# A macaron transformer block on one core: small VectorE intermediates put into the shared PSUM banks, and the plan of the order given new costs

## The reference

```python
x = x + 0.5 * ffn(layernorm(x), w_gate, w_up, w_down)
x = x + attn(layernorm(x), Wq, Wk, Wv, Wproj, lq1, lk1, lq2, lk2)
x = x + 0.5 * ffn(layernorm(x), w_gate, w_up, w_down)

# ffn, hidden width 704; q() is a blockwise FP4 quantise and dequantise over 16 features
h = silu(q(x) @ q(w_gate).T) * (q(x) @ q(w_up).T)
out = q(h) @ q(w_down).T
# q(): scale = max(max|block| / 6, 1e-12); round |v| / scale to 0, .5, 1, 1.5, 2, 3, 4, 6

# attn: differential attention, 8 heads, 2 x 8 query and key heads of width 16
q, k = rotary(rmsnorm(q)), rotary(rmsnorm(k))
a = softmax(causal(q @ k.T / 4))          # 16 maps of 2048 x 2048 for each batch
a = a[:, :, 0] - lam * a[:, :, 1]
out = layernorm(a @ v) * (1 - LAMBDA_INIT) @ Wproj.T    # layernorm over each head's 32
```

## Time and profile before

| what | value |
|---|---|
| three runs | 2467.5, 2468.85, 2469.09 us (median 2468.85) |
| the profiled execution, its own time | 2471.45 us |
| its span, first to last instruction | 2469.5 us |
| mean granted TensorE clock | 0.937 |
| instructions | 39323 |

### The profile page before, as it was taken

One profiled execution on the slowest core, in us unless ns is written; L12 is line 12 of the kernel. 1 busy time (PEld: TensorE's weight loads), 2 busy tenths in 40 slices (PEclk: granted clock), 3 DMA queues, 4 the chain that ended last, 5 costly groups with the idle time before them and its releaser, 6 DMA issues.

```text
span 2469.5 us, 39323 instructions
## 1 busy us (share of the span) xinstructions
PE 2099.7 (85%) x13502; PEld 839.6 (34%) x13502; DVE 1831.3 (74%) x3615; ACT 1777.8 (72%) x2660; POOL 1658.3 (67%) x1520
## 2 busy tenths in 40 slices
PE   1567999899897889899998889989898889998965
PEld 1233433233333333333333333333333333332322
DVE  6888787668758888777858888886867888873434
ACT  2345677978875778778786778877787677887852
POOL 3887666766756687876766677886776677862415
PEclk8788999999998999999998999999999999998986
DMA  3122322221312132232321322223241223221101
GB/s 92 34 40 55 65 49 49 47 53 30 68 39 52 19 63 50 56 66 44 55 58 19 53 48 63 60 33 71 33 84 21 47 32 79 49 50 34 33 1 41
DMA packets 409906, 119.36 MB, mean 48 GB/s; under 512 B 390638, under 2 KB 409454, under 8 KB 409710
## 3 DMA queue, kind: packets, MB, share of 16 engines
q1 hardware_dynamic: 409710, 116.86, 25.1%
HBM read 11.96 MB, written 8.39 MB: 8 GB/s over the span
## 4 chain that ended last, share of the span: by engine, by line
PE 45%; DVE 20%; ACT 8%; POOL 5%; issue 5%; DMA 2%; SPq 1%; ACTq 0%; DVEq 0%; POOLq 0%
PE psum_o L1365 11%; PE shared L1311 10%; PE shared L1324 7%; PE psum_s L1347 7%; ACT probs L1074 6%; PE shared L1332 4%; PE shared L1379 3%; DVE nwt L473 2%; DVE nwt L472 2%; DVE h L1166 1%; PE shared L1300 1%; DMA q_stack<-st_q 1%; DVE nwt L474 1%; POOL grid L965 1%; POOL hq L961 1%
## 5 line engine op out<-in xcount | busy, mean ns | idle before, releaser
L1074 ACT ACTIVATE probs<-psum_s 128x1024 f32<-128x1024 f32 (+3 forms) x1280 | 1092.0, 896 | 234.2 <-PE psum_s L1347 170.9
L1365 PE MATMUL psum_o<-probs,v_sb 128*32 128x512 f32 (+3 forms) x5120 | 590.6, 546 | 9.5 <-POOL probs L995 8.9
L1311 PE MATMUL shared<-w_gu_T,xT 128*128 128x480 f16 (+1 forms) x2304 | 522.6, 371 | 68.5 <-DMA xT<-x 44.4
L1347 PE MATMUL psum_s<-q_stack,k_stack 64*128 64x512 f16 (+3 forms) x2560 | 431.7, 359 | 113.6 <-ACT probs L1074 97.1
L1324 PE MATMUL shared<-w_down_T,hT 128*128 128x256 f16 (+1 forms) x2176 | 315.5, 292 | 77.3 <-DVE hq L1156 55.9
L1347 PEld LDWEIGHTS psum_s<-q_stack,k_stack 64*128 64x128 f16 x2560 | 110.1, 93 | 652.6 <-ACT probs L1074 465.9
L1311 PEld LDWEIGHTS shared<-w_gu_T,xT 128*128 128x128 f16 x2304 | 207.1, 99 | 352.7 <-issue 119.4
L995 POOL TENSOR_SCALAR_AFFINE_SELECT probs<-probs 128x512 f32<-128x512 f32 x256 | 172.6, 679 | 225.7 <-ACT probs L1074 224.4
L961 POOL TENSOR_TENSOR hq<-grid,hq 128x704 f32<-128x704 f32 x128 | 222.7, 1740 | 99.8 <-ACT grid L1019 99.7
L1009 ACT ACTIVATE hq<-shared,tanh_scale 128x240 f32<-128x240 f32 (+1 forms) x384 | 172.6, 454 | 155.7 <-PE shared L1311 143.9
L1324 PEld LDWEIGHTS shared<-w_down_T,hT 128*128 128x128 f16 (+1 forms) x2176 | 204.1, 103 | 193.5 <-issue 76.6
(11 more groups left out here) (120 smaller groups left out, 2848.2 us busy)
## 6 DMA issues: line engine op xcount, KB each, us to landing
xb<-L_attn_x SPq DMA_DIRECT2D x16, 512.0 KB, 4.0
out<-xb SPq DMA_DIRECT2D x16, 512.0 KB, 3.3
hT<-h SPq DMA_TRANSPOSE x128, 3.5
xT<-x SPq DMA_TRANSPOSE x64, 3.1
k_stack<-st_k SPq DMA_TRANSPOSE x64, 3.3
q_stack<-st_q SPq DMA_TRANSPOSE x64, 3.3
k_stack<-L_ffn_w_down SPq DMA_DIRECT2D x1, 704.0 KB, 8.7
k_stack<-L_ffn_w_gate SPq DMA_DIRECT2D x1, 480.0 KB, 4.6
```

What stands on the lines that cost most here:

```text
L1074: nc.scalar.activation(probs[:, s % 3, 2 * u:2 * u + 2, q0:CHUNK], psum_s[u][:, :, q0:CHUNK], ACT.Exp, scale=HD ** -0.5 / QK_SCALE ** 2).t ...
L1311: last = nc.tensor.matmul(bank(e)[:, 0:2 * (hi - lo)], xs[:, x, t % 2, k, :], w_gu_T[:, w, k, 2 * lo:2 * hi], start=n == 0, stop=n == len( ...
L1347: last = nc.tensor.matmul(psum_s[u][:, j, q0:CHUNK], k_stack[half, at, h, kt % NTC * P:(kt % NTC + 1) * P], q_stack[half, c % 2, h, q0:CHU ...
L1365: last = nc.tensor.matmul(psum_o[at:at + VD, q0:CHUNK], v_sb[:, kt // NTC % SLOTS * NTC + kt % NTC, 2 * g + u, :], probs[:, s % 3, 2 * u + ...
```

## The change

The costs and due times of the plan are replaced, and the model of time is refined: a stage may overlap a little with the next on its engine (`OVERLAP`), the way from one engine to another depends on the receiving one (`REACH`), TensorE's results come `DRAIN` later, and a switch between kinds of matmul tiling costs `SWITCH`. The stages `quant_x`, `quant_h`, `rms` and `head_stats` now take a shared bank each. In it stand the block maxima, and in the Newton stages `y` and `spread`; the products are reordered so that no instruction of `rsqrt` has both inputs in SBUF. `amax` and two slices of `nwt` go. `heads_out` multiplies its first half in place in the bank, only its second half goes to SBUF (`o_second`), the squares go back to the bank, and it is released by the last reduction. `head_stats` waits for its four `heads_out` through their banks. `norm_x` of a chunk comes after `norm_heads` of the chunk two earlier.

```diff
-DUE = dict(lead=57, spans=(23, 55, 57, 15), tail=50208, early=1.97, mlp1=(85, 27), qkv=(-162, 60), qk=(-77, 71), out=(-188, 149), mlp2=(99, 30),
+DUE = dict(lead=212, spans=(46, 134, 65, 12), tail=76515, early=0.23, mlp1=(30, 12), qkv=(-16, 71), qk=(-277, 221), out=(-819, 195), mlp2=(261, 40),
...
-            divide_h=1.45, divide_x=1.11, down=2.19, gate=0.82, grid_h=1.72, grid_x=1.33, head_stats=4.21,
-            heads_out=3.64, hidden=1.27, high_h=0.79, high_qk=1.14, high_x=0.63, low_h=1.18, low_qk=2.46,
...
-            project_out=1.09, project_qk=2.13, project_v=1.0, quant_h=1.83, quant_x=2.78, read_qk=0.6,
-            read_v=0.38, rms=7.63, rope=1.93, rope_add=1.38, rstd=2.9, square_h=1.61, square_x=1.29,
...
-START = 0.05
-LAG = 0.12
...
+            divide_h=1.46, divide_x=1.1, down=2.07, gate=0.82, grid_h=1.74, grid_x=1.37, head_stats=3.3,
+            heads_out=3.1, hidden=1.23, high_h=0.79, high_qk=1.14, high_x=0.63, low_h=1.23, low_qk=2.48,
...
+            project_out=0.87, project_qk=1.75, project_v=0.87, quant_h=1.68, quant_x=2.6, read_qk=0.59,
+            read_v=0.37, rms=4.3, rope=1.93, rope_add=1.32, rstd=2.7, square_h=1.61, square_x=1.29,
...
+OVERLAP = dict(tensor=0.0, vector=0.08, scalar=0.1, gpsimd=0.04, sync=0.0)
+REACH = dict(tensor=0.14, vector=0.04, scalar=0.04, gpsimd=0.08, sync=0.1)
+RELEASE = 0.06
+DRAIN = 0.14
+TILING = dict(scores=1, values=2)
+SWITCH = 0.11
...
-            free_at[engine] = start + weight
+            free_at[engine] = left[name] = start + weight - OVERLAP[engine]
+            if engine == "tensor":
+                tiling = TILING.get(name[0], 0)
             end[name] = start + weight + lands
             for n in needed_by[name]:
                 missing[n] -= 1
                 if not missing[n]:
-                    met[n] = max(end[m] + (LAG if self.stages[m][0] != self.stages[n][0] else 0)
-                                 for m in self.stages[n][3])
+                    met[n] = max(end[m] + REACH[self.stages[n][0]] if self.stages[m][0] != self.stages[n][0] else
+                                 left[m] for m in self.stages[n][3])
...
-        add(("quant_" + kind, *u), "vector", quant, due, needs, takes, frees)
+        q = ("quant_" + kind, *u)
+        add(q, "vector", quant, due, needs, [*takes, ("bank", q)], [*frees, ("bank", q)])
...
-            add(("norm_x", 1, t), "vector", .5, d, [("rstd", 1, c)], [("xrow", (1, t))],
+            add(("norm_x", 1, t), "vector", .5, d,
+                [("rstd", 1, c), ("norm_heads", NTC * (c - 2) - 1) if c >= 3 else None], [("xrow", (1, t))],
...
         add(("rms", c), "vector", 6.0, s0 + due["qk"][0] * k,
-            [*(("rope", t) for t in tiles), ("norm_qk", tiles[0] - 1) if c else None])
+            [*(("rope", t) for t in tiles), ("norm_qk", tiles[0] - 1) if c else None],
+            [("bank", ("rms", c))], [("bank", ("rms", c))])
...
-        add(("head_stats", c), "vector", 3.6, s0, [("heads_out", c, NG - 1), ("norm_heads", NTC * c - 1) if c else None])
+        add(("head_stats", c), "vector", 3.6, s0, [("heads_out", c, NG - 1), ("norm_heads", NTC * c - 1) if c else None],
+            [("bank", ("head_stats", c))], [("bank", ("head_stats", c))])
...
-        amax = sb("amax", [P, XU + HU, I // QB])
...
-        o_norm = sb("o_norm", [P, NTC, P])
+        o_second = sb("o_second", [P, NTC, 2 * VD])
...
-        def rsqrt(wait, done, dst, src, n):
-
-            half, y, t = (nwt[:, i, 0:n] for i in range(3))
+        def rsqrt(wait, done, dst, n, y, src):
+
+            half, t = (nwt[:, i, 0:n] for i in range(2))
...
-                wait(done(nc.vector.tensor_tensor(t, y, y, ALU.mult)))
-                wait(done(nc.vector.tensor_tensor(t, t, half, ALU.mult)))
-                b = done(nc.vector.scalar_tensor_tensor(dst if i == 2 else y, t, 1.5, y, ALU.add, ALU.mult))
-                wait(b)
-            return b
+                wait(done(nc.vector.tensor_tensor(t, half, y, ALU.mult)))
+                wait(done(nc.vector.tensor_tensor(t, t, y, ALU.mult)))
+                last = nc.vector.scalar_tensor_tensor(dst if i == 2 else y, t, 1.5, y, ALU.add, ALU.mult)
+                if i < 2:
+                    wait(done(last))
+            return last
...
-                    def block_scales(src, i, nb, floor):
-
-                        am, q, r = (ap[:, i, 0:nb] for ap in (amax, qscale, rscale))
-                        wait(done(nc.vector.tensor_reduce(am, by_block(src), AX_X, ALU.max,
-                                                          apply_absolute_value=True)))
-                        wait(done(nc.vector.tensor_scalar(q, am, SCALE_UP / 6.0, floor, ALU.mult, ALU.min)))
+                    def mine(e):
+
+                        if BANK[e][1]:
+                            dve.wait_ge(bank_free[BANK[e][0]], BANK[e][1])
+                        return bank(e)
+
+                    def block_scales(e, src, i, nb, floor):
+
+                        am, q, r = mine(e)[:, 0:nb], qscale[:, i, 0:nb], rscale[:, i, 0:nb]
+                        nc.vector.tensor_reduce(am, by_block(src), AX_X, ALU.max, apply_absolute_value=True)\
+                            .then_inc(full(e)[0], 1)
+                        dve.wait_ge(*full(e))
+                        nc.vector.tensor_scalar(q, am, SCALE_UP / 6.0, floor, ALU.mult, ALU.min).then_inc(read(e)[0], 1)
+                        dve.wait_ge(*read(e))
                         nc.vector.reciprocal(r, q).then_inc(scales_ready, 1)
...
-                            spread = nwt[:, 3, 0:n]
-
-                            wait(done(nc.vector.tensor_scalar(spread, ssq, 1.0 / (HD * QK_SCALE ** 2),
-                                                              RMS_EPS / QK_SCALE ** 2, ALU.mult, ALU.add)))
-                            rsqrt(wait, done, qk_rstd[:, :, :].rearrange("p a b -> p (a b)"), spread, n)
+                            y, spread = (mine(e)[:, i * n:(i + 1) * n] for i in range(2))
+                            nc.vector.tensor_scalar(spread, ssq, 1.0 / (HD * QK_SCALE ** 2), RMS_EPS / QK_SCALE ** 2,
+                                                    ALU.mult, ALU.add).then_inc(full(e)[0], 1)
+                            dve.wait_ge(*full(e))
+                            rsqrt(wait, done, qk_rstd[:, :, :].rearrange("p a b -> p (a b)"), n, y, spread)\
+                                .then_inc(read(e)[0], 1)
+                            dve.wait_ge(*read(e))
...
-                            nc.vector.tensor_tensor(
-                                o_norm[:, :, :].rearrange("p t (q d) -> p t q d", d=VD), rows,
-                                z_inv[:, :, :].unsqueeze(3).broadcast_to([P, NTC, 4, VD]), ALU.mult)\
-                                .then_inc(read(tr)[0], 1)
-                            dve.wait_ge(*read(tr))
+                            pairs = bank(tr)[:, :].rearrange("p (t f) -> p t f", f=4 * VD)
+                            second = o_second[:, :, :].rearrange("p t (q d) -> p t q d", d=VD)
+                            done(nc.vector.tensor_tensor(
+                                second, rows[:, :, 2:4], z_inv[:, :, 2:4].unsqueeze(3).broadcast_to([P, NTC, 2, VD]),
+                                ALU.mult))
+                            wait(done(nc.vector.tensor_tensor(
+                                rows[:, :, 0:2], rows[:, :, 0:2],
+                                z_inv[:, :, 0:2].unsqueeze(3).broadcast_to([P, NTC, 2, VD]), ALU.mult)))
                             to = heads[:, c % 2, :, g * 2 * VD:(g + 1) * 2 * VD]
                             if normed[0]:
                                 dve.wait_ge(xrow_normed, normed[0])
                             wait(done(nc.vector.scalar_tensor_tensor(
-                                to, o_norm[:, :, 2 * VD:4 * VD], neg_lam[:, 0:1], o_norm[:, :, 0:2 * VD],
-                                ALU.mult, ALU.add)))
+                                to, o_second[:, :, :], neg_lam[:, 0:1], pairs[:, :, 0:2 * VD], ALU.mult, ALU.add)))
 
                             by_head = to.rearrange("p t (h d) -> p t h d", d=VD)
                             wait(done(nc.vector.tensor_reduce(by_head[:, :, :, VD - 1], by_head[:, :, :, 0:VD - 1],
                                                               AX_X, ALU.add, negate=True)))
-                            o_sq = o_norm[:, :, 0:2 * VD]
+                            o_sq = pairs[:, :, 0:2 * VD]
                             wait(done(nc.vector.tensor_tensor(o_sq, to, to, ALU.mult)))
-                            done(nc.vector.tensor_reduce(head_ssq[:, c % 2, :, 2 * g:2 * g + 2],
-                                                         o_sq.rearrange("p t (h d) -> p t h d", d=VD),
-                                                         AX_X, ALU.add))
+                            nc.vector.tensor_reduce(head_ssq[:, c % 2, :, 2 * g:2 * g + 2],
+                                                    o_sq.rearrange("p t (h d) -> p t h d", d=VD),
```

(33 more changed lines are left out.)

31 lines of the change are left out of this document (18 added, 13 removed).

## The result

The changed kernel takes 2434.78 us (median of four runs, 2428.31 to 2437.81) against 2468.97 us for the kernel before: a ratio of 0.9858, 95% interval 0.9846 to 0.9871. That is 34 us, where 76 were forecast. The direction was right, and so was the wait for GpSimd; the size was not.

A forecast was written before the change was run, and what follows sets the result against it. No engine fills the span; TensorE comes nearest, its gaps hanging on VectorE's Newton stages, which wait for GpSimd. Terms -60 - 11 - 20 + 25 - 10 = -76 took 2471.45, less 2.6, to 2393 us; range 2335 to 2468.

The forecast's parts named there:

- the sign: VectorE's busy time in the changed kernel: near 1630 us expected, as one mark that the prediction holds.
- Term 1: Newton stages `rms` and `head_stats`: TensorE's idle time in their windows is won, -60 us (bounds -40 and -68).
- term 2: TensorE's clock after the gaps: six `down` stages no longer run at about 0.5, -11 us (bounds 0 and -11).
- term 4: Shared banks: VectorE takes one 224 times and waits 0.11 us on average, +25 us (0 to +112).
- Term 3: Block scales and `heads_out`: 79 us less VectorE work, a quarter counted as on the path, -20 us (0 to -40).
- TensorE gains new waits: Sign that the prediction is wrong: TensorE newly waits for `amax` or `heads_out` banks.
- banks decide: Rival, chance 0.14, slower: VectorE meets three taken banks, `gate` is late, gaps return; wait ahead of L1097; 2510 us.
- Term 5: New order of stages from new due times and costs: a small gain, -10 us (-40 to +40).
- given back: Rival, chance 0.20: the gaps close but the next wait, such as L1347's for ScalarE's `exp`, takes half; 2454 us.

The follow-up runs named there:

- two steps: Two Newton steps in place of three, in old or new order, with maxima and heads in a bank or without; four kernels, ratios 0.9758 to 0.9785 against the kernel before.

## Why the prediction was right or wrong

**What bounds the kernel: right.** VectorE's steps between SBUF operands waited for GpSimd, and gaps of TensorE hung on the Newton stages. With an operand in PSUM `rms` takes 4.05 to 4.06 us at any time (4.2 taken), `head_stats` 2.75 (3.2 taken). VectorE's busy time did not fall as far as the sign said, to 1679.5 us where near 1630 was foreseen. The Newton stages and the block scales gave back their 136 and 68 us, but `norm_qk`, `norm_heads` and the normalising in `quant_x` take 50 us more than before, and `heads_out`'s 13 us did not come.

**Terms 1 and 2, -71: too large by 39 us in the order that they were read from.** In the old order this placement brought 32. Term 1 counted as won nearly all of TensorE's idle time in the Newton windows, 60 of 68.2 us. In the run with that placement alone 47.6 us of it are still there, and over the whole span TensorE is idle 26 us less and busy 8 us less (2091.8 instead of 2099.7 us, for which term 2 had 11). What holds it up is what term 4 left out. The 69 us of the new order look like the forecast, but they are not its sum come true: the terms were read from the gaps of the old order, and in the new one the long stages hold up other work.

**Term 3, -20: right to a little low in the new order (21 + 10), nothing in the old one**, where the maxima alone measured 1.0006.

**Term 4, +25: this step failed.** It said that a free bank costs nothing and priced VectorE's wait for a bank, 0.11 us each at a use of 33%, since two of three are likely free. The cost is on the other side: TensorE waits for the bank that VectorE holds, 44.1 us in the old order for the Newton stages alone, with 32 of the 224 uses. An average over the span says nothing of it, because in the place shown above the other two banks are full just while VectorE is in its long stage. That holding the bank costs time is shown for the long stages: 81 us in the run that only held it. For the short ones no run prices it by itself, since none shortens them without a bank. An estimate in proportion to the time held, 108.9 against 210.8 us, gives 42 us, near the 39 that are missing. The sign *TensorE gains new waits* for these banks came true (25.5 and 5.2 us in the changed kernel). The rival *banks decide* had the place wrong in the same way as term 4: VectorE's idle time ahead of L1119 in the changed kernel is 12.3 us in 61 pieces behind its own `gate`, none over 0.2 us, and 2.5 us in 3 pieces behind `copy_xT`.

**Term 5, -10: the order gave nothing.** With equal placement old and new order are the same within 0.3% (0.9867 and 0.9858, 0.9785 and 0.9758 to 0.9774 with two steps). The idle time outside the Newton windows in the steady stretch, from which the term was bounded, was 133 us and not 118: only 52.5 of the 68.2 us lie in that stretch. In the new order TensorE waits 2.3 us for `qk_rstd` instead of 19.3, but its own waits are longer elsewhere. In the old order the books read: Newton stages -32, the other placements nothing, the order nothing, together about -34 where the sum had -76. Counted from the new order they read: placement -101, order +66, together -35. The new order is fitted to short stages and needs them.

The rival *given back*, 2454 at a chance of 0.20, came nearer in time (20 us off, the forecast 42) and in mechanism: part of what the gaps gave was taken by the next wait. That wait was not `exp`, which I named (97.1 us before, 92.4 after), but the bank. What in the new order costs the 66 us with everything in SBUF wasn't tried part by part; the waits for `copy_o` (48.0 us) and for `add_down` (34.6 us) are much longer than in the old order (5.1 and 20.0 us in all lines), which is a reading, not a test.

## What to carry to other kernels

When a slow engine's intermediates move into a buffer that it also has to empty for others, price the wait of the producer for that buffer, in the stretch where the engine is busy longest, not the average use. A placement and an order fitted to it should be measured apart: here each looked like 100 and 66 us in one frame and like 33 and 0 in the other, and only keeping an order to the stage told why. Shortening the chain by three instructions paid 26 us in the old order and 21 in the new one, nearly as much as the placement had (32 in the old). And a list of waits tells who ended them, not what a cause costs: 2.7 us of waits went with a gain of 21 us, and 124 us of new waits with a loss of 81.

## What the runs showed that was not expected

Waiting for GpSimd moves to the next instruction. In the old order with all placements, `norm_qk` and `norm_heads`, which still have both inputs in SBUF and come right behind the Newton stages, got slower at the same place in the order. Groups of the kernel before, then of that run:

```profile
L1221 DVE TENSOR_TENSOR roped<-roped,qk_rstd 128x512 f32<-128x512 f32 x64 | 55.7, 882 | 0.4
...
L1277 DVE TENSOR_TENSOR xrow<-heads,head_rstd 128x256 f32<-128x256 f32 x64 | 27.0, 453 | 6.8 <-PE shared L1300 6.2
```

```profile
L1267 DVE TENSOR_TENSOR roped<-roped,qk_rstd 128x512 f32<-128x512 f32 x64 | 62.7, 992 | 2.9 <-POOL roped L1003 2.4
...
L1327 DVE TENSOR_TENSOR xrow<-heads,head_rstd 128x256 f32<-128x256 f32 x64 | 48.7, 790 | 7.7 <-PE shared L1350 7.2
```

`norm_heads` went from 453 to 790 ns: 29 us of VectorE's saving came back in these two lines. The new order shows it with nothing changed but the place of the Newton stages: from the run with them back in SBUF to the changed kernel `norm_qk` went from 912 to 1131 ns and `norm_heads` from 505 to 745. In the long stage of the earlier trace rows GpSimd's last instruction had ended 1.1 us before the stage did, so what followed met nobody; that this is how it happens elsewhere too is argued from this one place.

The squares of `heads_out` (L1286, two inputs in SBUF) and the product just ahead (L1273, one input in PSUM) have the same size in the changed kernel. The first line's answer, with duration min/median/max:

```profile
L1286 DVE TENSOR_TENSOR shared<-heads x64: 432/746/1947, 260.5 to 2352.4; 128x256 f32<-128x256 f32 x64
```

and the second's:

```profile
L1273 DVE TENSOR_TENSOR shared<-shared,z_inv x64: 422/423/423, 259.1 to 2350.9; 128x256 f32<-128x256 f32 x64
```

The Trainium skill, SBUF — State Buffer, section Who interferes with whom, says that a VectorE instruction with two SBUF inputs contends with a GpSimd instruction that reads SBUF; by that rule the trace agrees, 432 to 1947 ns against 422 to 423, even with the output in PSUM. The Trainium skill, Perfetto Trace Analysis, section Optimizing Scalar/DVE Operations, gives VectorE about 60 ns of access cost on SBUF and 125 ns on PSUM. Such a fixed difference of 65 ns shows in no run here: a write is 295 against 287 ns. TENSOR_SCALAR instructions did get slower in PSUM, but with their columns: 264 ns at 44 columns, where the fastest from SBUF was 245, and 0.29 us at 128 columns, where it was 0.23.
